# A spectral-layer kernel: forward transform in parts on its own column tiles, inverse square roots by guess and corrections, and a new order of the engines' work

## The reference, cut to what matters

```python
h = layer_norm(x @ fc0_w + fc0_b)                   # 64 images of 64x64, 32 channels
for i in range(4):                                  # LAYERS
    x_ft = rfft2(h)                                 # 24 x 12 modes are kept
    out_ft[:, :, :12, :12]  = einsum('bixy,ioxy->boxy', x_ft[:, :, :12, :12], w1[i])
    out_ft[:, :, -12:, :12] = einsum('bixy,ioxy->boxy', x_ft[:, :, -12:, :12], w2[i])
    h = irfft2(out_ft) + einsum('bchw,oc->bohw', h, conv_w[i]) + conv_b[i]
    h = layer_norm(h, ln_g[i], ln_b[i])             # (h - mean) * rsqrt(var + eps) * g + b
    if i < 3: h = gelu(h)
h = fc3(gelu(fc2(gelu(fc1(h)))))                    # 64 tokens of 64
# then 77 text tokens are joined, and an attention block and an expert block follow
```

## Time and profile before

| | |
|---|---|
| median of 3 runs | 3192.75 us |
| profiled execution, its own time | 3191.55 us |
| its span, first to last instruction | 3189.8 us |
| TensorE busy | 2860.6 us (90%) |
| weight loads | 1963.0 us (62%) |
| VectorE busy | 2102.8 us (66%) |
| ScalarE busy | 2196.4 us (69%) |
| GpSimd busy | 2125.8 us (67%) |

### The profile page before, as it was taken

One profiled execution on the slowest core, in us unless ns is written; L12 is line 12 of the kernel. 1 busy time (PEld: TensorE's weight loads), 2 busy tenths in 40 slices (PEclk: granted clock), 3 DMA queues, 4 the chain that ended last, 5 costly groups with the idle time before them and its releaser, 6 DMA issues. The chain is left out here.

```text
span 3189.8 us, 199057 instructions
## 1 busy us (share of the span) xinstructions
PE 2860.6 (90%) x84638; PEld 1963.0 (62%) x84638; DVE 2102.8 (66%) x3768; ACT 2196.4 (69%) x3709; POOL 2125.8 (67%) x1147
## 2 busy tenths in 40 slices
PE   6777999997899998899999689999999968999997
PEld 4555777776677776677777434444444425666665
DVE  7765888883788886588888344444444437777775
ACT  4674777774677775577777267787787855666665
POOL 3773999993899996599999235445445425666663
PEclk9998999998999999899999789999999988999998
DMA  5774555554555554455555412112112111000000
GB/s 165 222 228 151 178 180 179 181 181 143 155 178 175 187 175 156 138 180 180 181 174 165 136 45 61 58 53 62 58 53 62 48 32 36 14 13 13 13 13 10
DMA packets 215411, 369.30 MB, mean 116 GB/s; under 512 B 116050, under 2 KB 133266, under 8 KB 215010
## 3 DMA queue, kind: packets, MB, share of 16 engines
q1 hardware_dynamic: 203602, 353.37, 35.4%
q10 hardware_dynamic: 7920, 10.03, 1.0%
q0 software_dynamic: 3744, 3.84, 0.9%
HBM read 209.43 MB, written 157.71 MB: 115 GB/s over the span
## 5 line engine op out<-in xcount | busy, mean ns | idle before, releaser
L1484 POOL TENSOR_TENSOR rstd<-var,mhalf 128x16 f32<-128x16 f32 x512 | 1525.0, 2996 | 635.8 <-DVE var L1241 631.7
L1255 DVE TENSOR_TENSOR zt<-ps,rstd 128x512 f32<-128x512 f32 x512 | 345.4, 684 | 150.3 <-POOL rstd L1484 142.5
L617 PEld LDWEIGHTS ps<-d,hp 128*32 128x32 f32 x24576 | 293.0, 111 | 130.9 <-ACT hp L918 92.2
L617 PE MATMUL ps<-d,hp 128*32 128x48 f32 x24576 | 345.8, 209 | 20.9 <-ACT hp L918 5.3
L546 PEld LDWEIGHTS ps<-cwl,hc 64*64 64x64 f32 x16384 | 298.3, 139 | 95.7 <-issue 80.8
L529 PE MATMUL ps<-zb,ex 48*64 48x512 f32 x2048 | 291.1, 637 | 67.9 <-DVE zb L1324 26.4
L557 PEld LDWEIGHTS ps<-dyi,gt 64*48 64x48 f32 x16384 | 231.5, 124 | 168.3 <-issue 156.4
L1241 DVE TENSOR_REDUCE var<-sq 128x16 f32<-128x528 f32 x384 | 267.6, 698 | 90.5 <-ACT sq L907 88.1
L907 ACT ACTIVATE sq<-ps 128x512 f32<-128x512 f32 x384 | 237.4, 648 | 125.3 <-PE ps L546 121.9
L1077 ACT ACTIVATE a<-ps,fc1b 128x1024 f32<-128x1024 f32 x256 | 271.3, 1111 | 64.3 <-PE ps L820 64.3
L557 PE MATMUL ps<-dyi,gt 64*48 64x32 f32 x16384 | 274.0, 210 | 45.0 <-ACT gt L972 17.6
(11 more groups left out here) (199 smaller groups left out, 4845.4 us busy)
## 6 DMA issues: line engine op xcount, KB each, us to landing
h_scratch<-ho SPq DMA_DIRECT2D x256, 512.0 KB
hc<-h_scratch SPq DMA_DIRECT2D x256, 512.0 KB, 3.9
wsb<-in_w SPq DMA_DIRECT2D x64, 288.0 KB
gin<-g_scratch SPq DMA_DIRECT2D x252, 72.0 KB
gin<-g_scratch SPq DMA_DIRECT2D x504, 36.0 KB
g_scratch<-hp ACTq DMA_DIRECT2D x32, 192.0 KB, 4.5
g_scratch<-hp SPq DMA_DIRECT2D x32, 192.0 KB, 3.6
tokens<-wsb SPq DMA_DIRECT2D x256, 4.0 KB
```

The lines of the kernel that those rows point to most:

```text
L617: last = nc.tensor.matmul(a_ps[row:row + 32, 2 * TRIG * k:2 * TRIG * k + 2 * TRIG], hp[b][:, u, 8 * j + k].rearrange("p v r -> p (v r)"), ...
L1255: nc.vector.tensor_tensor(by_px(zt[h][:, u]), by_px(main_ps(s, h, u)), scale, ALU.mult).then_inc(norm_ready, 1)
L1484: nc.gpsimd.tensor_tensor(rstd[u][:], var[u][:], mhalf[:], ALU.pow).then_inc(rstd_ready, 1)
```

## The change

- `f1` has 24 moving columns (d1 without the doubling) and fills the bank a_ps with 16 channels, so that two runs and two copies serve a pair in place of four; asb is one buffer, 128x768, of which the second buffer's place stays as gsx, for the mix. `f2` takes 128x32 weights and makes the parts in their own column tiles: 48 matmuls a pair, four tiles, the table cy with two sets of 24 columns. The mixing weights' and the stem's layouts follow; the stem's f1_x and f2_x change in the same way, and modes_out becomes one matmul of 288 columns.
- The power on GpSimd is replaced: VectorE makes a first guess of 1/sqrt by integer arithmetic on the bits of the sums, for a half's two units in one operation, and GpSimd corrects it in ten operations on 128x32, each of which waits for the semaphore of the one before.
- ScalarE copies both halves of the inverse transform (z_copy); VectorE's copy falls away.
- The order of a step changes on TensorE (f2 in one run, i1 in one run ahead of f1, f1 in two), on ScalarE (both coefficient copies behind the squares, transposes' copies and gelus in the odd half) and on VectorE (both normalisings together, both sums and the guess together, then gain and bias of both units).

```diff
+MAGIC = float(0x5f3759df)
-        asb = [sb(f"asb{p}", [128, 2 * KX, C, 2]) for p in range(2)]
+        asb = sb("asb", [128, C, TRIG])
+        gsx = sb("gsx", [128, 1536])
-        var = [sb(f"var{u}", [128, 16]) for u in range(2)]
-        rstd = [sb(f"rstd{u}", [128, 16]) for u in range(2)]
+        var = [sb(f"var{h}", [128, 2, 16]) for h in range(2)]
+        rstd = [sb(f"rstd{h}", [128, 2, 16]) for h in range(2)]
+        near, ratio = (sb(n, [128, 2, 16]) for n in ("near", "ratio"))
...
             def f1(s, b, g, j):
-                pe.wait_ge(a_ready, 4 * rank(s, g) + j)
-                for k in range(8):
+                pe.wait_ge(a_ready, 2 * rank(s, g) + j)
+                for k in range(CH):
                     for a in range(2):
                         for u in range(2):
                             row = 64 * a + 32 * u
-                            last = nc.tensor.matmul(a_ps[row:row + 32, 2 * TRIG * k:2 * TRIG * k + 2 * TRIG],
-                                                    hp[b][:, u, 8 * j + k].rearrange("p v r -> p (v r)"),
-                                                    d1[:, a].rearrange("p x s -> p (x s)"),
+                            last = nc.tensor.matmul(a_ps[row:row + 32, TRIG * k:TRIG * k + TRIG],
+                                                    hp[b][:, u, CH * j + k].rearrange("p v r -> p (v r)"), d1[:, a],
                                                     start=True, stop=True, tile_position=(0, row))
...
+            def f2(s, g):
+                pe.wait_ge(a_ready, 2 * rank(s, g) + 2)
+                at_least(pe, x_ready, rank(s, g))
+                for m in range(2):
+                    for a in range(6):
+                        o = KY * (6 * m + a)
+                        for c in range(2):
+                            for n in range(2):
+                                row = 64 * c + 32 * n
+                                last = nc.tensor.matmul(x_ps[row:row + 32, o:o + KY], asb[:, :, KX * m + 2 * a + c], cy[:, n],
+                                                        start=True, stop=True, tile_position=(0, row))
+                last.then_inc(x_psr, 1)
...
                     if older:
                         with where_older(g):
                             turn(s, 0, g - 2, 1, 1)
-                            f2(s, 0, g - 2, 0)
+                            f2(s, g - 2)
+                    if here:
+                        widen(s, 0, g, 1)
+                        conv(s, 0, g, 1)
                     if old:
                         turn(s, 0, g - 1, 0, 0)
+                    if here:
+                        with where_next(g):
+                            i1(s, g + 1, 0, 16)
                     if old:
                         turn(s, 0, g - 1, 0, 1)
+                        f1(s, 0, g - 1, 0)
                     if old:
-                        f1(s, 0, g - 1, 0)
+                        turn(s, 0, g - 1, 1, 0)
+                        f1(s, 0, g - 1, 1)
...
             def even(i, p):                              # ScalarE
                 square(s, here[0], 0, 0)
                 square(s, here[0], 0, 1)
                 coefficients(s, nxt[0], 0)
+                coefficients(s, nxt[0], 1)
                 x_copy(s, older[0])
+                hc_copy(s, older[0], 1, 1)
             def odd(i, p):                               # ScalarE
                 square(s, here[0], 1, 0)
                 square(s, here[0], 1, 1)
+                gelu(s, old[0], 1, 0)
+                hc_copy(s, old[0], 0, 0)
+                gelu(s, old[0], 1, 1)
+                hc_copy(s, old[0], 0, 1)
+                z_copy(s, nxt[0], 0)
+                a_copy(s, old[0], 0)
                 hc_copy(s, old[0], 1, 0)
+                z_copy(s, nxt[0], 1)
+                a_copy(s, old[0], 1)
                 gelu(s, here[0], 0, 0)
                 gelu(s, here[0], 0, 1)
...
+            def guess(s, g, h):                          # VectorE
+                dve.wait_ge(var_ready, 4 * rank(s, g) + 2 * h + 2)
+                nc.vector.tensor_scalar(rstd[h][:].bitcast(I32), var[h][:].bitcast(I32), -0.5, MAGIC, ALU.mult, ALU.add
+                                        ).then_inc(guess_ready, 1)
             def even(i, p):                              # VectorE
                 normalise(s, *old, 0)
+                normalise(s, *old, 1)
+                reduce(s, *here, 0)
+                reduce(s, *here, 1)
+                guess(s, *here)
                 gain(s, *old, 0)
                 bias(s, *old, 0)
+                gain(s, *old, 1)
+                bias(s, *old, 1)
             def odd(i, p):                               # VectorE
+                reduce(s, *here, 0)
+                reduce(s, *here, 1)
+                guess(s, *here)
                 normalise(s, *old, 0)
+                normalise(s, *old, 1)
                 gain(s, *old, 0)
                 bias(s, *old, 0)
                 gain(s, *old, 1)
                 bias(s, *old, 1)
                 if here and p == 0:
                     w_sum(s, i)
...
-            def rstds(s, g, h, u):
-                pool.wait_ge(var_ready, 4 * rank(s, g) + 2 * h + u + 1)
-                nc.gpsimd.tensor_tensor(rstd[u][:], var[u][:], mhalf[:], ALU.pow).then_inc(rstd_ready, 1)
+            def rstds(s, g, h):
+                q = 2 * rank(s, g) + h
+                x, y, gp = var[h][:], rstd[h][:], nc.gpsimd
+                def closer_by(k, *ins):
+                    ins[0].then_inc(closer, 1)
+                    pool.wait_ge(closer, 9 * (q - 2 * PAIRS) + k)
+                    if k in (2, 4, 8):
+                        waits_apart(pool, passed)
+                pool.wait_ge(rstd_ready, q)
+                pool.wait_ge(guess_ready, q + 1 - 2 * PAIRS)
+                closer_by(1, gp.tensor_tensor(ratio[:], y, y, ALU.mult))
+                closer_by(2, gp.tensor_tensor(ratio[:], ratio[:], x, ALU.mult))
+                closer_by(3, gp.tensor_scalar(near[:], ratio[:], -5.0 / 3, None, ALU.add))
+                closer_by(4, gp.tensor_tensor(near[:], near[:], near[:], ALU.mult))
+                closer_by(5, gp.tensor_scalar(near[:], near[:], 3.0 / 8, 5.0 / 6, ALU.mult, ALU.add))
+                closer_by(6, gp.tensor_tensor(near[:], near[:], y, ALU.mult))
+                closer_by(7, gp.tensor_tensor(ratio[:], near[:], near[:], ALU.mult))
+                closer_by(8, gp.tensor_tensor(ratio[:], ratio[:], x, ALU.mult))
+                closer_by(9, gp.tensor_scalar(ratio[:], ratio[:], -0.5, 1.5, ALU.mult, ALU.add))
+                gp.tensor_tensor(y, ratio[:], near[:], ALU.mult).then_inc(rstd_ready, 1)
```

More of the change, by code:

```diff
@@ L247, in token_network @@
         z_psr = sem("z_psr")
-        zb_ready = [sem(f"zb_ready{c}") for c in range(2)]
+        zb_ready = sem("zb_ready")
         zl_psr = sem("zl_psr")
@@ L522, in widen @@
                     else:
-                        for c in range(2):
-                            pe.wait_ge(zb_ready[c], rank(s, g) - PAIRS + 1)
+                        pe.wait_ge(zb_ready, 2 * (rank(s, g) - PAIRS) + 2)
                 waits_apart(pe, passed)
@@ L688, in modes_out @@
                 at_least(pe, x_ready, g)
-                pe.wait_ge(a_ready, min(g + 2, PAIRS) if isinstance(g, int) else g + 2)
-                for m in range(2):
-                    k = slice(64 * m, 64 * m + 32 + 2 * XCH)
-                    last = nc.tensor.matmul(xs_ps[:, m, :], f0x[k, 1, :], xk[k], start=True, stop=True, tile_position=(64 * m, 0))
-                last.then_inc(x_psr, 1)
+                nc.tensor.matmul(x_ps, f0x[:, 1, :], xk, start=True, stop=True).then_inc(x_psr, 1)
             def stem():
@@ L1108, in _ @@
                     coefficients(s, 0, c)
-                z_copy(s, 0)
+                for c in range(2):
+                    z_copy(s, 0, c)
                 layer(s)
@@ L1505, in step @@
                     if behind(i, p, h, 0, 2):
-                        for u in range(2):
-                            rstds(s, 2 * i + p, h, u)
+                        rstds(s, 2 * i + p, h)
                         if p == 0 and h == 1 and not final:
@@ L2208, in layouts @@
                     f0x[[32 * n + 8 * a + 2 * k + b, 64 + 32 * n + 8 * a + 2 * k + b], 0, a, :, b] = f4[k]
-                    f0x[64 * n + 32 * a + 2 * k + b, 1, a, :, b] = f4[k]
-    out["fc0x"] = f0x.reshape(128, 2, 4 * C)
+    for q in range(4):
+        f0q[q, 0:XCH, q] = f4
+    f0x = f0x.reshape(128, 2, 4 * C)
+    f0x[:, 1] = f0q.reshape(128, 4 * C)
+    out["fc0x"] = f0x
     out["conv_b"] = np.tile(f("L0_tok_conv_b")[None], (64, 1, 1))
```

183 lines of the change are left out of this document (61 added, 122 removed).

## The result

The changed kernel takes **3282.34 us** (median of 4 runs, 3278.45 to 3289.17) against 3193.47 us of the kernel before, run beside it: a ratio of 1.0279, 95% interval 1.0253 to 1.0305. Forecast were 3122 us, a range of 2985 to 3215 and 0.18 for slower. The profiled execution has a span of 3282.4 us, 92.6 more than before's 3189.8.

A forecast was written before the change was run, and what follows sets the result against it. The ring of VectorE and GpSimd was to bound the layers, cutting the pitch from 14.18 to 13.45 us over 90 pairs: -66; drains -9, stem +5, constants +1, last pass 0. From 3191.55: 3122 us, range 2985 to 3215.

The forecast's parts named there:

- the moves: Layers' queues: coefficient copies stand right behind the squares, so SP's row loads issue earlier and nothing on SP comes later.
- 0.3 us of hand-overs: TensorE in the layer: 0.3 us a pair for waits on copies, since a_ps and the transposes' bank are single.
- rival: Alternatives: TensorE binds, 3001 us, chance 0.20; dear small matmuls, 3218, 0.05; dear GpSimd steps, 3245, 0.13; no change, 3204, 0.13.
- The ring of VectorE and GpSimd: Layers: sums, guess, GpSimd's scale chain and normalising wait on each other; 10.25 + 8r = 13.45 us a pair, setting the pitch.
- r: Time of one chained short GpSimd step in the scales, with its gap: 0.40 us, bounds 0.33 to 0.53.
- TensorE idle over 1 us a pair: Layers: sign of a right forecast, TensorE idling before the widening because the VectorE and GpSimd ring is longer.
- The port: Layers: beside VectorE's gain and bias, GpSimd gets one step through per VectorE operation, some 0.72 us.
- the dear end: TensorE in the layer: 14.5 us a pair if new f1 and f2 cost 15 ns a record, against 12.1 at 8.3.
- same weight shape: Reason for pricing new f1 and f2 at 8.3 ns a record, from the attention's 32-column weights; 15 kept as upper end.
- Drains: End of each layer: two f1-copy hand-overs instead of four, about -3 us each, -9 in all.
- Stem and constants: Before the layers: stem's f2_x doubling to 96 records, +5 us, and one more short chain before the start, +1.
- Last pass: Last pass: the scales' guess, chain and hand-overs, 4.4 us, fit the present 4.7 and 4.5 us; change 0.

The follow-up runs named there:

- kernel 1: Changed kernel with SP's six row loads issued ahead of both stores of h: 3098.79 us, ratio 0.9703 to the kernel before the change.
- 2: Changed kernel with ScalarE's copies of the modes and of the transposes' bank ahead of the coefficient copies again: 3164.95 us, ratio 0.9901 to the kernel before.
- 8: Kernel before the change, with only the six row loads moved ahead of the two stores of h: 3202.27 us, ratio 1.0026 to the unedited kernel before.
- kernel 9: Changed kernel with the row loads placed between the two stores of h: 3092.6 us, ratio 0.9671 to the kernel before the change.
- 11: Changed kernel with row loads between the stores and GpSimd's second correction left out (six steps): 3079.34 us, ratio 0.963 to the kernel before.
- 12: Changed kernel with row loads between the stores, f2's weights contiguous by strided PSUM reads, and six GpSimd steps: 3021.72 us, ratio 0.9461 to the kernel before.
- experiment 3: Changed kernel with f2's weights contiguous, the copy writing strided: 3278.07 us, ratio 1.0264 to the kernel before the change.
- kernel 10: Changed kernel with row loads between the stores and f2's weights contiguous by strided PSUM reads, ten GpSimd steps: 3092.06 us, ratio 0.9677 to the kernel before.
- kernel 7: Changed kernel with row loads ahead of both stores and the ten GpSimd steps replaced by two powers a half: 3482.1 us, ratio 1.0919 to the kernel before.

## Why the prediction was wrong

**The step that failed** is the sentence on the moves: "SP's six row loads ... are issued earlier, in SP's old order behind the loads of h; nothing on SP comes later." It followed the coefficient copies, which do move forward, and asked what they release. It did not follow the two copies of half 0's transposes, which the new order moves from ScalarE's even half step to its odd one, and of which the second is what SP's store waits for. The row loads stand behind that store. So they came 3.3 us later with respect to the squares (3.6 us ahead instead of 6.9), while the coefficient copies became due sooner. The next sentence, that the copy which frees the bank "ends about as TensorE's second convolution does: it is in the 0.3 us of hand-overs", fell with it: the convolution of the traced pair ends at 577.12, the copy at 578.80. No rival had this ring; all of them argued over prices. Experiments 1 and 2 show it, and 8 shows that the same move gains nothing in the kernel before.

**The rest of the sum held in part.** With the loads out of the ring the kernel takes 3099 us where the working gives 3122. That they lie so near is partly luck: the ring was sized 0.5 us a pair too long, f2 was priced too low, which the ring beside it hid, and the drains' gain did not come.

- The ring of VectorE and GpSimd: forecast 13.45 us with r = 0.40. A step that runs beside nothing takes 0.35 us (562.14 to 563.54 below, four steps); at 0.35 the formula gives 10.25 + 2.8 = 13.05, and the pitch is 12.88 to 12.96 with the ring among the limits. The size of r was a little high, at the middle of its bounds. That the ring alone sets the pitch, with TensorE idle over 1 us a pair, was not so: in kernel 9 TensorE is idle 9.6 of 280 us, 0.4 us a pair.
- The port. Beside gain and bias a step takes as long as one VectorE operation, forecast 0.72 us, measured (569.24 - 567.29) / 3 = 0.65; in the chain ahead of these rows, from 558.90 to 561.84, four steps take 0.74 us each. GpSimd of the changed kernel, a chain beside nothing, then one beside gain and bias; and VectorE in the second stretch:

```profile
562.14 0.25 POOL L1475 TENSOR_TENSOR near<-near,rstd 128x32 f32<-128x32 f32 x1
562.47 0.24 POOL L1476 TENSOR_TENSOR ratio<-near 128x32 f32<-128x32 f32 x1
...
563.54 0.26 POOL L1479 TENSOR_TENSOR rstd<-ratio,near 128x32 f32<-128x32 f32 x1
...
567.29 0.51 POOL L1474 TENSOR_SCALAR near<-near 128x32 f32<-128x32 f32 x1 [0.20 <-POOL near L1473]
567.88 0.57 POOL L1475 TENSOR_TENSOR near<-near,rstd 128x32 f32<-128x32 f32 x1
568.53 0.63 POOL L1476 TENSOR_TENSOR ratio<-near 128x32 f32<-128x32 f32 x1
569.24 0.26 POOL L1477 TENSOR_TENSOR ratio<-ratio,var 128x32 f32<-128x32 f32 x1
```
```profile
567.64 0.70 DVE L1299 TENSOR_TENSOR zt<-zt,gbx 128x512 f32<-128x512 f32 x1
568.37 0.69 DVE L1306 TENSOR_TENSOR zt<-zt,gbx 128x512 f32<-128x512 f32 x1
568.98 0.74 DVE L1331 TENSOR_REDUCE wmean<-wsb 128x18 f32 x1
```

  As soon as VectorE is on a sum with one input (568.98), the step is back at 0.26. The Trainium skill's page SBUF — State Buffer (Who interferes with whom) describes this as an exclusive lock that is held for a whole instruction, against GpSimd, by a VectorE operation with two SBUF inputs too; the trace agrees (0.65 us a step beside such operations, 0.35 beside none).
- TensorE: forecast 12.1 us a pair, 14.5 at the dear end. f1 came out as taken: (1.18 - 0.11) / 127 = 8.4 ns a record. f2 did not: (1.66 - 0.16) / 95 = 15.8 ns where 8.3 was taken and 15 kept as the upper end; with contiguous weights it is (0.91 - 0.11) / 95 = 8.4. So the reason for the choice, "same weight shape", looked at the shape and not at the layout. Where TensorE and its hand-overs pace the kernel (kernels 11 and 12), the pitch is 12.75 with that f2 and 12.22 with the dense one, against the forecast 12.1. Weight loads of the changed kernel, then of experiment 3:

```profile
569.20 1.18 PEld L619 LDWEIGHTS ps<-d,hp 128*32 128x32 f32 x128
...
573.41 1.66 PEld L634 LDWEIGHTS ps<-cy,asb 128*32 128x32 f32 x96
```
```profile
564.89 0.91 PEld L634 LDWEIGHTS ps<-cy,asb 128*32 128x32 f32 x96
```

  By the floor in the Trainium skill's page TensorE: Matmul & The Clock Gate (Part 1) f1 and f2 would have taken 8.8 us a pair, an estimate; they take 2 x 1.28 + 1.76 = 4.3, so the floor does not hold for these matmuls on column tiles.
- Drains, -9 us: not there. From a layer's last centring to the next one's first, the stretch grew by 4.4 and 2.1 us, and in kernel 1 too it is 3.3 and 0.7 us longer than before. Stem and constants, +6: the first layer's first centring comes 5.6 us later in the changed kernel and 3.5 in kernel 1. Last pass, 0: from the last centring to the end +3.9 us in the changed kernel, -3.2 in kernel 1.

For kernel 1 the parts add up to 3.5 - 104.4 + 4.0 - 3.2 = -100.1 us, but for rounding the difference of the spans (3089.8 - 3189.8); the -104.4 are its three layers, in place of the forecast -66 and -9.

## What to carry to other kernels

When an order is rewritten, follow every moved instruction to all that waits for it, and on an in-order queue to what stands behind the waiter: here a copy moved by half a step held a store, and the store held six loads that have nothing to do with it. When all engines become less busy and the time grows, look for the ring in the list of waits: a wait once in every pair for a transfer, and another engine's wait once in every pair for the waiter. And before a term is tuned, see what stands next to it: two limits near 12.8 us hid each other, and taking away either alone was worth next to nothing.

## What the runs showed of the hardware

A weight load of 128x32 whose columns lie 96 bytes apart takes 163 ns in the mean and one of contiguous columns 109, and a run of such matmuls 15.8 ns a record against 8.4 (experiment 3). Writing the contiguous layout cost ScalarE about as much as it saved TensorE, 2 x 0.35 against 0.75 us a pair: the copy of 128x384 from PSUM takes 479 ns when it writes in order, 830 when consecutive elements go 128 bytes apart, and 478 when it reads PSUM strided and writes in order (experiment 3 and kernel 10):

```profile
L935 ACT COPY asb<-ps 128x384 f32<-128x384 f32 x48 | 23.0, 478 | 10.7 <-PE ps L619 10.4
```

The Trainium skill's page SBUF — State Buffer (Door 1: The DMA port swizzle) says that SBUF has lines of 16 bytes and that each access which crosses to a new line pays a penalty; the strided weight loads and the strided copy agree with it in direction, and the prices above are this case's.

Powers of 128x16 take 3042 ns each in a layer of kernel 7; the ten short operations that replace two of them take 0.22 to 0.26 us each beside nothing.

TensorE's granted clock in the changed layer is 0.93 in the mean (a mix of its two levels, 1.2 and 2.4 GHz), where it was 0.99, with a wait in every pair; with the loads first it is 0.98 over the same stretch. So the lower clock came and went with the ring. It is not what makes the layers longer to begin with: the pair traced above ran at the upper level throughout (1.00 below) and took 14.73 us. So did 46 pairs of the three layers, counted from coefficient copy to coefficient copy, with 14.7 us each in the mean against before's 14.18. The 38 that the lower level touched took 15.1, so part of the loss goes with the clock; how much of that is its cause and how much its effect is not shown.

```profile
567.75:582.48 14.73, 12.58 (x686) 10.67 (x680) 10.42 (x18) 10.40 (x21) 9.01 (x23) 1.00 0.57 162
```
